# First layer of a two-layer cross attention: both turned blocks of a pair ahead of the value products, third turning bank from the start, sums read elsewhere, large loads spread

## The chip, the cores and the metric

One NeuronCore of a Trainium2 chip runs the whole program. The metric is the device time of one launch in microseconds (us). TensorE (PE) multiplies and transposes, VectorE (DVE), ScalarE (ACT) and GpSimd (POOL) do the elementwise work, SyncE (SP) issues nearly all the transfers. TensorE's clock is granted at one of two levels, 1.2 or 2.4 GHz, and the trace tells which.

## The reference

Two sequences (B = 2) of 512 tokens by 512 features attend to 1024 context tokens each. First comes a grouped-query layer with 32 query heads, 8 key/value heads and a head size of 16:

```python
q = hidden @ Wq + bq; k = enc @ Wk + bk; v = enc @ Wv + bv
scores = einsum('bkgld,bksd->bkgls', q, k) * scale + mask
out = einsum('bkgls,bksd->bkgld', softmax(scores), v)
x = out @ Wo + bo + hidden          # then layer norm, gamma, beta
```

Then follow two cross attentions of 16 heads of size 128 with layer norms and an MLP of 2048. The change touches only the first, grouped-query layer and the transfers that run beside it.

## The kernel before

The kernel is one program with its order written out by hand for every engine; semaphores tie the engines together. Each of the two sequences ("batch" in the code) passes through three stages: projections of the first layer, its attention loop, and then the two large attentions and the MLP. The loop of the first layer begins 36.0 us after the span's start and the first output product (L1269) ends it at 288.4 us; for the second sequence these are 1335.2 and 1588.7 us.

**The attention loop.** It has 128 steps (STEPS0). A step is 128 query rows of two key/value heads stacked in the row halves of the array against 1024 context tokens. 8 steps are a unit (UNIT), 4 steps a group (GROUPS), 2 steps a pair. For each step t:

- `scores0(r)` (L1193) makes the scores of steps 2r and 2r+1 into the two 2-bank tiles `ps_s[0]` and `ps_s[1]`. It first waits for `max0_done`, that is until DVE has read both tiles of the pair before.
- `maxima0(t)` on DVE (L1676) adds the mask, writes `sm` and takes the row extreme.
- `exp0(t)` on ACT (L815) writes `p0` and the row sum.
- `turned0(t)` on PE (L1212) transposes the 128x1024 block in 16 row-tiled pieces of 64 rows into two PSUM banks, half q=0 and half q=1. Three banks are there for it (`turn_banks`: `ps_t[0]`, `ps_t[1]`, `ps_m[1]`), and `bank_of_half` deals them out in turn. Before it starts, PE waits for both its banks to have been copied out (`t0_copied`).
- `copied0(t, q)` copies a half from PSUM to `pt0`: q=0 on ACT (L723 in the trace, a helper), q=1 on DVE (L1684).
- `values0` (L1229) multiplies the turned blocks of a whole group by V, in quarters i = 0 to 3, two quarters in each pair, for the group before the one being turned.

At the end of a unit PE also transposes the inverse sums (L1236), ACT copies them (`rb0`, L723), and DVE's `normalised(u)` (L1696) writes `aT0`; the next unit's first value product waits for that (`a0_done`).

**The order in one pair (t odd, r = (t-1)/2).** PE: `scores0(r+1)`, `turned0(t-1)`, two quarters of `values0`, `turned0(t)`. DVE: `maxima0(t+1)`, at one place `normalised`, `maxima0(t+2)`, `copied0(t-1,1)`, `copied0(t,1)`. ACT: `copied0(t-1,0)`, `exp0(t+1)`, `copied0(t,0)`, `exp0(t+2)`, and once a unit the copy of the inverse sums. In the first four steps (`h < UNIT`) only two of the three banks are used, since `ps_m[1]` still holds a part of the query projection (`bank0[5]`), which DVE evacuates with `low_part(5)` in step t = 1.

**Queues beside it.** SP issues, in order: the scratch writes and stack reads of q and k, then `x_res` (1 MB) and a row, `w0o` (1 MB), `acc` (0.5 MB), and the 16 `wob` tiles (0.5 MB each, two buffers), of which the third waits for POOL's sums. POOL adds the row to `x_res` in unit 2 and then scales and sums the `wob` tiles (`value_rows`, as many in a unit as `ROWS_OF_UNIT` says); each unit it also spreads the inverse sums (L613).

Of the kernel before, what the change touches and what calls it, by code (L numbers as in the profile page):

```python
# [29 lines left out]
KVH, GROUPS, HD = 8, 4, 16  # L30
# [14 lines left out]
UNIT = 2 * GROUPS  # L45
UNITS0 = KVP * LT
STEPS0 = UNITS0 * UNIT
# [4 lines left out]


P_Q = (2, 3, 4, 5)
ROWS_OF_UNIT = (0, 0, 0, 1, 1, 1, 2, 1, 1, 2, 1, 1, 2, 1, 1, 1)
assert sum(ROWS_OF_UNIT) == LAYERS * PAIRS and len(ROWS_OF_UNIT) == UNITS0
U_PROJ0, U_MLP = 6, 2 * FPAIRS
U_B = U_PROJ0 + LT + U_MLP
# [30 lines left out]
def build(nc, d):  # L89

    with ExitStack() as ctx:
# [142 lines left out]
        bank_free = sem("bank_free")  # L234
# [7 lines left out]
        w0o_in = sem("w0o_in")  # L242
# [43 lines left out]

        rows1 = (row, row1)

        bank0 = [ps_m[0][:], ps_m[1][:], ps_s[0][:, 0:512], ps_s[1][:, 0:512], ps_m[0][:], ps_m[1][:]]
        turn_banks = [*ps_t, ps_m[1]]  # L290
        bank_of_half = [h % 2 if h < UNIT else (0, 1, 2, 0, 2, 1, 0, 2)[h % 8] for h in range(2 * STEPS0)]

        def half0(t, q):

# [11 lines left out]
        def inverse0(u):  # L306

            return ps_m[0][:, u % 2 * 2 * P + P:u % 2 * 2 * P + 2 * P]
# [51 lines left out]
        def _(sp):  # L360
# [8 lines left out]
            def load_wob(b, f):  # L369
                if f >= 2:  # L370
                    sp.wait_ge(acc_done, (b * V_B + f - 1) * 2)
                    apart()
                sp.dma_start(wob[f % 2][:], d["wo"][f, :, :, :]).then_inc(wob_in[f % 2], 16)
# [28 lines left out]
            def batch(b, last):  # L402
# [12 lines left out]
                for i in range(4):  # L415
# [11 lines left out]
                    if i == 1:  # L427
                        for k in range(2):
                            sp.wait_ge(scr_k_out[k], 16 * (b + 1))
                            apart()  # L430
                            stack_k(sp, k, slice(1, KVP), stack_rest)

                sp.dma_start(x_res[:], d["x"][b, :, :, :]).then_inc(xres_in, 16)
                load_row(b * ROWS, 0)
                sp.dma_start(w0o[:], d["w0o"]).then_inc(w0o_in, 16)

                def load_wv(f):
                    load_vo(b * VO_B + 2 * f, d["wv"][f, :, :].rearrange("p (s n) -> p s n", s=2))
# [8 lines left out]
                def move_turned(x, m):  # L447
# [5 lines left out]
                    for j in range(4):  # L453
                        for a in range(4):
                            sp.dma_start(f32(pT[1][32 * a:32 * a + 32, j, :]),  # L455
                                         pb[32 * j:32 * j + 32, a, :]).then_inc(moved_in[j], 16)

                sp.dma_start(acc[:], d["rows1"]).then_inc(acc_in, 16)
                for f in range(V_B):
                    load_wob(b, f)  # L460
                load_wqk(0)
                load_wv(0)
# [59 lines left out]
        def _(pool):  # L522
# [63 lines left out]
            def batch(b, last):  # L586
# [11 lines left out]

                u0 = b * UNITS0
                for u in range(UNITS0):  # L600
                    if u == 2:
                        pool.wait_ge(xres_in, 16 * (b + 1))
                        pool.wait_ge(row_in, 16 * (2 * b + 1))
                        add_row()
                        pool.wait_ge(acc_in, 16 * (b + 1))
                        pool.wait_ge(const_in, 16 * 5)
                    for i in range(ROWS_OF_UNIT[u]):
                        value_rows(sum(ROWS_OF_UNIT[:u]) + i)

                    pool.wait_ge(rz0_done, u0 + u + 1)  # L610
                    if u >= 2:
                        pool.wait_ge(rb0_filled, u0 + u - 1)
                    nc.gpsimd.tensor_tensor(r0[u % 2][:], rz0[:, u % 2, :].unsqueeze(2).to_broadcast([P, UNIT, HD]),  # L613
                                            zero[:].unsqueeze(2).to_broadcast([P, UNIT, HD]), ALU.add)\
                        .then_inc(r0_done, 1)
# [105 lines left out]
        def _(act):  # L721
            def copy(out, in_):
                return nc.scalar.activation(out, in_, ACT.Copy)  # L723
# [60 lines left out]
            def batch(b, last):  # L784
# [22 lines left out]
                def exp0(t):  # L807
                    u, i = t // UNIT, t % UNIT
                    if t >= 2:
                        act.wait_ge(t0_filled[1], t0 + t - 1)  # L810
                    if t % UNIT == 0 and u >= 2:
                        act.wait_ge(rz0_done, b * UNITS0 + u - 1)
                    act.wait_ge(max0_done, t0 + t + 1)
                    col = i % GROUPS * 2 + i // GROUPS
                    nc.scalar.activation(p0[t % 2][:], sm[t % 2][:], ACT.Exp, bias=nm0[:, t % 2:t % 2 + 1],  # L815
                                         scale=-1.0, accum_out=z0[:, u % 2, col:col + 1]).then_inc(exp0_done, 1)
# [11 lines left out]
                for t in range(1, STEPS0, 2):  # L828
                    copied0(t - 1, 0)
                    if t + 2 < STEPS0:  # L830
                        exp0(t + 1)
                    copied0(t, 0)
                    if t + 2 < STEPS0:
                        exp0(t + 2)
                    if t % UNIT == GROUPS - 1 and t > UNIT:
                        u = t // UNIT - 1
                        act.wait_ge(rb0_filled, b * UNITS0 + u + 1)
                        copy(rb0[u % 2][:], inverse0(u)).then_inc(rb0_done, 1)
                act.wait_ge(rb0_filled, b * UNITS0 + UNITS0)
                copy(rb0[1][:], inverse0(UNITS0 - 1)).then_inc(rb0_done, 1)  # L840
                act.wait_ge(row_added, b * ROWS + 2)
# [224 lines left out]
        def _(pe):  # L1066
# [23 lines left out]
            def free(n):  # L1090
                pe.wait_ge(bank_free, n + 1)
# [23 lines left out]
            with pe.Fori(0, B) as b:  # L1115
# [29 lines left out]
                def project_q0(i):  # L1145
                    if i == 0:
                        pe.wait_ge(batch_done, b + 1)
                    if i >= 2:
                        free(nb + i)
                    for c in range(CT):  # L1150
                        mm = passes(bank0[P_Q[i]], lambda x, _: query_weights(x, i)[:, c, :],
                                    lambda y, _: hT[y][:, c, :], 1, start=c == 0, stop=c == CT - 1)
                    mm.then_inc(bank_filled, 1)
# [22 lines left out]


                pe.wait_ge(stack_in, 16 * 18 * (b + 1))
                pe.wait_ge(bank_free, nb + 6)
                pe.wait_ge(v32_done, b * 3 + 3)  # L1180
                apart()

# [17 lines left out]
                def turned0(t):  # L1200
                    pe.wait_ge(exp0_done, t0 + t + 1)
                    for q in range(2):
                        before = half_before(t, q)
                        if before is not None:
                            pe.wait_ge(t0_copied[before[1]], t0 + before[0] + 1)
                        elif bank_of_half[2 * t + q] == 2:
                            pe.wait_ge(bank_free, nb + U_PROJ0 + 2)
                    apart()
                    for st in range(ST):
                        for q in range(2):  # L1210
                            rows = slice(TILE * q, TILE * q + TILE)
                            mm = nc.tensor.transpose(half0(t, q)[:, st * TILE:(st + 1) * TILE],  # L1212
                                                     p0[t % 2][rows, st * P:(st + 1) * P], ident[rows, rows])
                            if st == ST - 1:
                                mm.then_inc(t0_filled[q], 1)
# [27 lines left out]
                for r in range(1, PAIRS0):  # L1243
                    t = 2 * r + 1
                    if r + 1 == PAIRS0 // KVP:
                        pe.wait_ge(stack_rest, 16 * 30 * (b + 1))
                    if r + 1 < PAIRS0:
                        scores0(r + 1)
                    turned0(t - 1)
                    if t >= GROUPS:  # L1250
                        for i in (t % GROUPS - 1, t % GROUPS):
                            values0(t // GROUPS * GROUPS - GROUPS, i)
                    turned0(t)
                for i in range(4):
                    values0(STEPS0 - GROUPS, i)

# [278 lines left out]
        def _(dve):  # L1535
# [8 lines left out]
            def apart():  # L1544

                dve.sem_inc(apart_dve, 1)
# [89 lines left out]
            def batch(b, last):  # L1636
# [21 lines left out]
                    low_part(i)  # L1658
                for i in range(2):
                    values_in(i)  # L1660
                for i in range(3, 5):
                    low_part(i)


# [28 lines left out]
                def normalised(u):  # L1693
                    kp, lt = divmod(u, LT)
                    dve.wait_ge(rb0_done, u0 + u + 1)
                    nc.vector.tensor_tensor(aT0[:, kp, lt * P:(lt + 1) * P], unit0(u), rb0[u % 2][:],  # L1696
                                            ALU.mult).then_inc(a0_done, 1)
# [3 lines left out]
                for t in range(1, STEPS0, 2):  # L1701
                    if t + 1 == UNIT:
                        dve.wait_ge(mask_rest, 16 * (b + 1))
                        apart()
                    if t + 2 < STEPS0:
                        maxima0(t + 1)
                    if t % UNIT == GROUPS + 1 and t > UNIT:
                        normalised(t // UNIT - 1)
                    if t + 2 < STEPS0:
                        maxima0(t + 2)  # L1710
                    copied0(t - 1, 1)
                    copied0(t, 1)
                    if t == 1:
                        low_part(5)
                    if t % UNIT == UNIT - 1:
                        inverse(t // UNIT)
                normalised(UNITS0 - 1)
# [333 lines left out]
```

## Time and profile before

| | |
|---|---|
| Runs before (3) | 2613.81, 2618.31, 2618.70 us; median 2618.31 |
| Profiled execution | 2616.33 us, of which the span is 2614.3 us |
| Busy share of the span | PE 96%, weight loads 79%, DVE 65%, ACT 57%, POOL 50% |
| Mean granted TensorE clock | 0.989 of full |

Busy shares are averages over stages with different limits: in the large attentions PE hardly pauses, in the first layer it does. The page is therefore read by stage.

### The profile page before, as it was taken

The page shows a single profiled execution, that of the slowest core. Times are in us where ns is not written, and L with a number is a line of the kernel's source. Part 1 is how long each engine was busy: PE and PEld are TensorE (multiplying, and loading weights), DVE is VectorE, ACT ScalarE, POOL GpSimd, SP SyncE. Part 2 cuts the span into 40 slices and gives each one's busy share as a digit, 9 for nine tenths or more (in the row PEclk, how much of TensorE's full clock was granted, in tenths as well). Part 3 has the DMA queues.
Part 4 walks back from the last instruction along what each step waited for, and adds up shares of the span by engine and source line. Part 5 has one row for each costly group of instructions (what it writes and reads, how often), then busy time and mean ns, then how long its engine had stood idle before and what let it go on. Part 6 is the DMA issues. An engine that isn't in the chain of part 4 may idle for free. (4 is left out here: it accounts for less than half of the span.)

```text
span 2614.3 us, 53032 instructions
## 1 busy us (share of the span) xinstructions
PE 2497.5 (96%) x19480; PEld 2063.8 (79%) x19480; DVE 1711.2 (65%) x2600; ACT 1495.2 (57%) x2360; POOL 1310.0 (50%) x746
## 2 busy tenths in 40 slices
PE   6888999999999999999978889999999999999999
PEld 5666688888888888888866666888888888888887
DVE  5999776656657656665269996665666576666541
ACT  5899455555445555545458994555554555554543
POOL 1244246666544666555603433466655446665644
PEclk8999999999999999999989999999999999999999
DMA  7312125354423445442472110334545133544522
GB/s 216 92 58 69 34 71 127 98 124 131 101 73 83 115 103 132 118 113 70 153 173 76 53 67 33 94 104 112 130 111 121 52 99 99 126 128 103 132 71 64
DMA packets 83649, 263.57 MB, mean 101 GB/s; under 512 B 20096, under 2 KB 24336, under 8 KB 77088
## 3 DMA queue, kind: packets, MB, share of 16 engines
q1 hardware_dynamic: 82496, 260.80, 37.6%
q8 instruction: 114, 1.87, 0.3%
q10 hardware_dynamic: 992, 0.52, 0.1%
q14 instruction: 47, 0.39, 0.0%
HBM read 135.39 MB, written 8.40 MB: 55 GB/s over the span
## 5 line engine op out<-in xcount | busy, mean ns | idle before, releaser
L537 POOL TENSOR_TENSOR pT_lo<-pT_lo,pT_hi 128x1024 fp32r<-128x1024 f32 x220 | 529.2, 2406 | 502.2 <-ACT pT_hi L723 496.3
L723 ACT ACTIVATE pT_hi<-pT_lo 128x1024 fp32r<-128x1024 f32 x224 | 237.8, 1062 | 327.4 <-DMA pT_lo<-pb 327.4
L862 ACT ACTIVATE p<-ps_s,nm 128x1024 f32<-128x1024 f32 x256 | 284.7, 1112 | 205.5 <-DVE nm L1755 204.9
L1752 DVE TENSOR_REDUCE nmx<-ps_s 128x1 f32<-128x1024 f32 x256 | 309.7, 1210 | 121.9 <-PE ps_s L1071 121.9
L1071 PE MATMUL ps_s<-kT,qT 128*128 128x512 f32 x1536 | 383.6, 392 | 0.0
L1771 DVE STREAM_TRANSPOSE pb<-p 128x1024 f32<-128x1024 f32 x224 | 278.2, 1242 | 105.8 <-ACT p L862 101.6
L1071 PEld LDWEIGHTS ps_s<-kT,qT 128*128 128x128 f32 x1536 | 281.3, 188 | 55.4 <-ACT p L862 1.0
L1676 DVE CUSTOM_DVE_ANT_0 sm<-ps_s,mask 128x1024 f32<-128x1024 f32 x256 | 305.4, 1213 | 19.5 <-PE ps_s L1193 15.5
L815 ACT ACTIVATE p<-sm,nm 128x1024 f32<-128x1024 f32 x256 | 293.2, 1145 | 19.1 <-DVE nm L1676 15.3
L1071 PE MATMUL ps_t<-ctxT,wa 128*128 128x512 f32 x1080 | 255.9, 390 | 0.0
L1071 PE MATMUL ps_m<-hT,wa 128*128 128x512 f32 x1008 | 243.5, 393 | 0.7 <-ACT g L1033 0.7
L1071 PEld LDWEIGHTS ps_t<-ctxT,wa 128*128 128x128 f32 x1080 | 202.9, 188 | 43.1 <-issue 1.0
L537 POOL TENSOR_TENSOR wa<-stg_qk,wa 128x1024 fp32r<-128x1024 f32 x80 | 190.8, 2403 | 70.3 <-ACT wa L723 70.2
L1071 PEld LDWEIGHTS ps_m<-hT,wa 128*128 128x128 f32 x1008 | 187.4, 188 | 46.3 <-issue 7.0
L1071 PEld LDWEIGHTS ps_t<-wv,ctxT 128*128 128x128 f32 x1728 | 212.7, 188 | 6.9 <-DVE pT_lo L1761 1.1
L1071 PE MATMUL ps_t<-wv,ctxT 128*128 128x256 f32 x1728 | 215.6, 280 | 0.0
L1212 PE MATMUL ps_t<-ident,p 64*128 64x64 f32 x2608 | 188.0, 235 | 17.6 <-DVE pt L1684 10.9
L1212 PEld LDWEIGHTS ps_t<-ident,p 64*128 64x128 f32 x2608 | 154.9, 145 | 57.8 <-issue 54.0
L613 POOL TENSOR_TENSOR r<-rz,zero 128x128 f32<-128x128 f32 x32 | 12.7, 398 | 352.9 <-issue 223.6
L537 POOL TENSOR_TENSOR v<-proj,v 128x512 fp32r<-128x512 f32 x128 | 164.8, 1298 | 40.9 <-ACT v L723 40.6
L1229 PE MATMUL ps_m<-pt,v 128*32 128x128 f32 x4096 | 142.9, 280 | 37.4 <-DVE aT L1696 29.9
L1336 PE MATMUL ps_m<-pT_hi,v 128*128 128x512 f32 x512 | 163.8, 391 | 2.9 <-POOL pT_lo L537 2.4
(181 smaller groups left out, 4664.2 us busy)
## 6 DMA issues: line engine op xcount, KB each, us to landing
pT_lo<-pb SPq DMA_DIRECT2D x896, 128.0 KB, 2.3
stg_qk<-in_wqk SPq DMA_DIRECT2D x40, 1024.0 KB, 7.4
stg_vo<-in_wo SPq DMA_DIRECT2D x48, 512.0 KB, 3.6
wob<-in_wo SPq DMA_DIRECT2D x32, 512.0 KB, 3.6
stg_vo<-in_wv SPq DMA_DIRECT2D x32, 512.0 KB, 3.6
q_stack<-scr_q SPq DMA_DIRECT2D x48, 128.0 KB, 4.2
st_ctx<-in_ctxT SPq DMA_DIRECT2D x8, 512.0 KB, 6.2
scr_q<-parts SPq DMA_DIRECT2D x8, 512.0 KB, 6.2
```

The lines of the kernel that those rows point to most:

```text
L537: return nc.gpsimd.tensor_tensor(out, x, f32(hi), ALU.subtract)
L613: nc.gpsimd.tensor_tensor(r0[u % 2][:], rz0[:, u % 2, :].unsqueeze(2).to_broadcast([P, UNIT, HD]), zero[:].unsqueeze(2).to_broadcast([P, U ...
L723: return nc.scalar.activation(out, in_, ACT.Copy)
L815: nc.scalar.activation(p0[t % 2][:], sm[t % 2][:], ACT.Exp, bias=nm0[:, t % 2:t % 2 + 1], scale=-1.0, accum_out=z0[:, u % 2, col:col + 1]) ...
L862: nc.scalar.activation(p[t % 2][:], ps_s[t % 2][:], ACT.Exp, bias=nm[:, i:i + 1], scale=SCALE1, accum_out=sums[:, i:i + 1]).then_inc(exp_d ...
L1071: mm = nc.tensor.matmul(out, lhs(x, c), rhs(y, c), start=start and c == 0 and i == 0, stop=stop and c == n_tiles - 1 and i == 2)
L1212: mm = nc.tensor.transpose(half0(t, q)[:, st * TILE:(st + 1) * TILE], p0[t % 2][rows, st * P:(st + 1) * P], ident[rows, rows])
L1229: mm = nc.tensor.matmul(unit0(u)[gr * 2 * HD:(gr + 1) * 2 * HD, :], v32[:, st, 2 * kp + gr % 2, cols_v], pt0[(t + gr) % RING][:, st, :], s ...
L1336: mm = nc.tensor.matmul(bank1(n)[:].rearrange("p (j n) -> p j n", j=4), v[a][:, st, h * P:(h + 1) * P], moving[c](st), start=st == 0 and i ...
L1676: nc.vector.tensor_tensor_reduce(sm[i][:], ps_s[i][:], mask[:, lt, :], -1.0, 3.0e38, ALU.add, ALU.min, nm0[:, i:i + 1]).then_inc(max0_done, 1)
L1752: nc.vector.tensor_reduce(nmx[:, i:i + 1], ps_s[t % 2][:], AX.X, ALU.max, negate=True)\
L1771: nc.vector.transpose(pb[:].rearrange("p a (s n) -> p s a n", s=ST)[:, :, :, lt * 32:(lt + 1) * 32], p[t % 2][:].rearrange("p (s a n) -> p ...
```

## The change

- The parts of the query projection that were made in `ps_m[0]` and `ps_m[1]` (`bank0[4]`, `bank0[5]`) are made in the second halves of `ps_s[0]` and `ps_s[1]`. The loop's first scores wait for all six parts to be read, `low_part(5)` moves ahead of the loop, and all three turning banks are used from the first step.
- PE turns both blocks of a pair one after the other and then does the value products.
- `normalised(u)` and ACT's copy of the inverse sums are placed in another round of the loop: `normalised` one pair earlier, after the copies, and the ACT copy ahead of `exp0(t+2)`.
- SP holds `x_res` and its row back until 4 groups are done, `acc` and the first `wob` until 6, the second `wob` until 7, and `w0o` goes between the fourth and the fifth `wob`. POOL adds the row in unit 3 and its sums are dealt out a little later.

```diff
-ROWS_OF_UNIT = (0, 0, 0, 1, 1, 1, 2, 1, 1, 2, 1, 1, 2, 1, 1, 1)
+ROWS_OF_UNIT = (0, 0, 0, 0, 1, 1, 2, 1, 2, 1, 2, 1, 2, 1, 1, 1)
-        bank0 = [ps_m[0][:], ps_m[1][:], ps_s[0][:, 0:512], ps_s[1][:, 0:512], ps_m[0][:], ps_m[1][:]]
+        bank0 = [ps_m[0][:], ps_m[1][:], ps_s[0][:, 0:512], ps_s[1][:, 0:512],
+                 ps_s[0][:, 512:1024], ps_s[1][:, 512:1024]]
-        bank_of_half = [h % 2 if h < UNIT else (0, 1, 2, 0, 2, 1, 0, 2)[h % 8] for h in range(2 * STEPS0)]
+        bank_of_half = [(0, 1, 2, 0, 2, 1, 0, 2)[h % 8] for h in range(2 * STEPS0)]
...
+                def after_group(n):
+                    sp.wait_ge(pv0_done, b * (STEPS0 // GROUPS) + n)
+                    apart()
+
+                after_group(4)
                 sp.dma_start(x_res[:], d["x"][b, :, :, :]).then_inc(xres_in, 16)
                 load_row(b * ROWS, 0)
-                sp.dma_start(w0o[:], d["w0o"]).then_inc(w0o_in, 16)
...
+                after_group(6)
                 sp.dma_start(acc[:], d["rows1"]).then_inc(acc_in, 16)
                 for f in range(V_B):
+                    if f == 1:
+                        after_group(7)
+                    if f == 4:
+                        sp.dma_start(w0o[:], d["w0o"]).then_inc(w0o_in, 16)
                     load_wob(b, f)
...
-                    if u == 2:
+                    if u == 3:
                         pool.wait_ge(xres_in, 16 * (b + 1))
...
                     copied0(t, 0)
-                    if t + 2 < STEPS0:
-                        exp0(t + 2)
                     if t % UNIT == GROUPS - 1 and t > UNIT:
                         u = t // UNIT - 1
                         act.wait_ge(rb0_filled, b * UNITS0 + u + 1)
                         copy(rb0[u % 2][:], inverse0(u)).then_inc(rb0_done, 1)
+                    if t + 2 < STEPS0:
+                        exp0(t + 2)
...
-                    if i >= 2:
-                        free(nb + i)
...
-                pe.wait_ge(bank_free, nb + 6)
+                pe.wait_ge(bank_free, nb + U_PROJ0 + 2)
...
                     turned0(t - 1)
+                    turned0(t)
                     if t >= GROUPS:
                         for i in (t % GROUPS - 1, t % GROUPS):
                             values0(t // GROUPS * GROUPS - GROUPS, i)
-                    turned0(t)
...
-                for i in range(3, 5):
+                for i in range(3, 6):
                     low_part(i)
...
-                    if t % UNIT == GROUPS + 1 and t > UNIT:
-                        normalised(t // UNIT - 1)
                     if t + 2 < STEPS0:
                         maxima0(t + 2)
                     copied0(t - 1, 1)
                     copied0(t, 1)
-                    if t == 1:
-                        low_part(5)
+                    if t % UNIT == GROUPS - 1 and t > UNIT:
+                        normalised(t // UNIT - 1)
```

## Rows read from the trace of the kernel before

**Rows 1.** Stretches: us from:to, length, busy us (count) by engine, PE clock, DMA.

```profile
119.70:134.30 14.60, 12.58 (x275) 9.27 (x273) 14.38 (x26) 13.50 (x26) 4.83 (x4) 1.00 0.12 39
...
36.00:288.40 252.40, 210.36 (x4373) 154.60 (x4374) 232.14 (x417) 218.14 (x401) 81.75 (x65) 0.95 0.29 79
1335.10:1588.70 253.60, 210.81 (x4373) 155.24 (x4374) 231.91 (x417) 218.32 (x401) 81.79 (x65) 0.95 0.29 79
```

**Rows 2.** Order of time, DVE: start us, us, engine, line, operation, count, [idle before].

```profile
119.71 0.69 DVE L1684 COPY pt<-ps_t 128x512 f32<-128x512 f32 x1 [0.18 <-PE ps_t L1212]
...
126.30 1.28 DVE L1684 COPY pt<-ps_t 128x512 f32<-128x512 f32 x2
...
129.79 0.68 DVE L1684 COPY pt<-ps_t 128x512 f32<-128x512 f32 x1
...
132.12 0.28 DVE L1696 TENSOR_TENSOR aT<-ps_m,rb 128x128 f32<-128x128 f32 x1
...
134.33 0.69 DVE L1684 COPY pt<-ps_t 128x512 f32<-128x512 f32 x1 [0.18 <-PE ps_t L1212]
```

**Rows 3.** Order of time, TensorE: scores, turned blocks and value products at full clock.

```profile
59.47 0.73 PE L1193 MATMUL ps_s<-k_stack,q_stack 48*128 48x512 f32 x4
60.27 0.71 PE L1212 MATMUL ps_t<-ident,p 64*128 64x64 f32 x16
...
127.88 1.08 PE L1229 MATMUL ps_m<-pt,v 128*32 128x128 f32 x32
128.90 0.33 PE L1236 MATMUL ps_m<-ident,r 128*128 128x128 f32 x1
...
133.48 0.27 PE L1212 MATMUL ps_m<-ident,p 64*128 64x64 f32 x1
...
134.98 0.24 PE L1212 MATMUL ps_m<-ident,p 64*128 64x64 f32 x1 [0.27 <-issue]
...
135.62 1.08 PE L1229 MATMUL ps_m<-pt,v 128*32 128x128 f32 x32
```

**Rows 4.** Order of time, ACT, the same stretch.

```profile
134.28 0.60 ACT L723 ACTIVATE pt<-ps_m 128x512 f32<-128x512 f32 x1 [0.74 <-PE ps_m L1212]
```

**Rows 5.** Who waited for whom, 90 to 270 us: us in total, times, longest.

```profile
PE ps_m L1229 <- DVE aT L1696: 11.9, 12, 1.0
```

**Rows 6.** Order of time, TensorE at half clock, first pairs and just behind the stall.

```profile
44.55 1.12 PE L1212 MATMUL ps_t<-ident,p 64*128 64x64 f32 x16 [2.65 <-DVE pt L1684]
...
51.46 1.23 PE L1193 MATMUL ps_s<-k_stack,q_stack 48*128 48x512 f32 x4
52.72 1.11 PE L1212 MATMUL ps_t<-ident,p 64*128 64x64 f32 x16
53.77 1.08 PE L1229 MATMUL ps_m<-pt,v 128*32 128x128 f32 x16
...
79.74 1.93 PE L1229 MATMUL ps_m<-pt,v 128*32 128x128 f32 x32
81.60 0.37 PE L1212 MATMUL ps_m<-ident,p 64*128 64x64 f32 x1
```

**Rows 7.** Order of time, ACT at the loop's start.

```profile
41.93 0.60 ACT L723 ACTIVATE pt<-ps_t 128x512 f32<-128x512 f32 x1 [0.89 <-PE ps_t L1212]
...
53.84 0.60 ACT L723 ACTIVATE pt<-ps_t 128x512 f32<-128x512 f32 x1 [0.37 <-PE ps_t L1212]
```

**Rows 8.** Order of time, TensorE at the one long stall.

```profile
76.22 0.64 PE L1229 MATMUL ps_m<-pt,v 128*32 128x128 f32 x2 [2.95 <-issue]
```

**Rows 9.** Stretches around the stall and around 1577 us, columns as in Rows 1.

```profile
76.00:78.00 2.00, 1.78 (x20) 1.40 (x22) 0.00 (x0) 0.01 (x1) 0.00 (x0) 0.50 0.98 401
...
1578.00:1580.00 2.00, 2.00 (x40) 1.53 (x34) 1.37 (x3) 0.77 (x2) 0.00 (x0) 0.50 0.00 0
```

**Rows 10.** Order of time, TensorE at the end of the loop.

```profile
276.11 0.73 PE L1193 MATMUL ps_s<-k_stack,q_stack 48*128 48x512 f32 x4
...
288.37 13.90 PE L1269 MATMUL ps_m<-w0o,aT 128*128 128x512 f32 x32
```

More of the change, by code:

```diff
@@ L1205, in turned0 @@
                             pe.wait_ge(t0_copied[before[1]], t0 + before[0] + 1)
-                        elif bank_of_half[2 * t + q] == 2:
-                            pe.wait_ge(bank_free, nb + U_PROJ0 + 2)
                     apart()
```

## The prediction

> **What bounds the kernel now.** The change touches only the first layer's loop, so the page's shares (PE 96% over the span) say nothing about it. I read the table of stretches first: the two loops take 252.4 and 253.6 us, together 506 of 2614 [rows 1]. In a steady unit of 8 steps DVE is busy 14.38 of 14.60 us, ACT 13.50, PE 12.58 [rows 1]. So DVE sets the pace there, ACT is close and PE has the most room. The order of time on DVE confirms it. A unit runs from the copy at 119.71 to the copy at 134.33, that is 14.62 us. An undisturbed pair is 129.79 - 126.30 = 3.49 us (two copies start 0.60 apart, two maxima 1.15 apart) [rows 2]. Four such pairs make 13.96; with the reciprocal of the sums (about 0.12) and the normalising step (start to start 0.21, busy 0.28 [rows 2]) a unit needs 14.29. DVE therefore waits some 0.33 us in each unit, and all of it lies in the pair behind `normalised`, where PE has stood 1.0 us waiting for `a0_done`, 12 times in the steady stretch [rows 5].
>
> Three things are lost outside the steady units. With two banks, the second turned block waits 2.65 us for a DVE copy [rows 6], and one pair later it happens again. At 73.3 us PE stands still for 2.95 us with nothing to wait for that the trace shows, while the transfers move some 400 GB/s, and its clock is then granted at 0.50, that is 1.2 GHz, for about 7 us [rows 8, 9]. And the first 19 us of the loop run at 1.2 GHz: a turned block takes 1.11 us there and 0.71 later [rows 3, 6].
>
> **The changed order on PE, the largest term.** What has to be asked is what `turned0(t)` waits for. With the pattern (0, 1, 2, 0, 2, 1, 0, 2), two blocks turned together need four halves and only three banks exist. For every odd t the half q=1 gets the very bank that the half q=0 of t-1 has just used: half 3 takes bank 0 again behind half 0, half 7 takes bank 2 behind half 4. So the second block of a pair always waits until ACT has copied a half of the first one. Before, two quarters of the value products (1.08 us) lay between the two blocks and covered that round trip. Now nothing does, and the value products come behind it.
>
> The chain of one pair at full clock, start to start:
> - scores to the first turned block: 60.27 - 59.47 = 0.80 [rows 3]
> - that block to ACT's copy of it: 134.28 - 133.48 = 0.80, a case where ACT was waiting [rows 3, 4]
> - the copy to the next turned block: 134.98 - 134.28 = 0.70 (0.60 of copy and 0.10 of signal) [rows 3, 4]
> - the turned block to the value products: 135.62 - 134.98 = 0.64 [rows 3]
> - the value products to what follows: 128.90 - 127.88 = 1.02, with 1.08 busy [rows 3]; I take 1.05 for the scores that follow now.
>
> The sum is 3.99 us. Without the round trip it was 0.80 + 0.64 + 1.05 + 0.76 = about 3.25, below DVE's 3.49. At 3.99 PE's chain is the longest. DVE needs 3.49 and ACT 3.24 (two copies at 0.49 start to start, two exponentials at 1.13, which run without a gap in most pairs), so ACT is free when the first block is ready and adds nothing, and the two row maxima of a pair are read 3.3 us after its scores began, before the 3.99 are over. Once a unit the transpose of the inverse sums adds 0.26 start to start (0.33 busy [rows 3]). A unit is 4 x 3.99 + 0.26 = 16.22 us against 14.62: +1.6.
>
> The link from value products to scores occurs nowhere in the trace. Its lower bound is a start 0.2 before the last products end; its upper bound is their whole 1.08 and the 0.09 that stand between the scores' end and the next block (0.80 less 0.71). With the other links the pair comes to 3.8 to 4.1.
>
> **The sums in another round.** ACT's copy of the inverse sums (0.15 start to start) and `normalised` (0.21) keep their cost. The wait of 1.0 us for `a0_done` [rows 5] goes: `normalised` is done about 5 us after the pair's scores, and the value product that needs it starts 7 us after them. This would be worth the 0.33 us a unit if DVE were the bound. PE being the bound, it is already in the chain above, which holds no such wait. ACT now waits for the transpose ahead of `exp0(t+2)`, about 1 us; ACT has 0.75 us a pair to spare, and `exp0(t+2)` is asked for only 1.5 us after the next pair's first block. Cost nothing; with no cover, at most 0.3 us a unit.
>
> **Third bank at once.** The second block then starts behind ACT's copy (41.93 + 0.70 = 42.6) and not at 44.55 [rows 6, 7]. The third pair's scores start when DVE has read the second pair, about 0.9 us (a copy and its signals) before that 44.55: at 43.7. From there the chain without value products, 1.26 + 1.12 + 0.70 and about 0.85 from the second block to the scores (links below), brings the fourth pair's scores at 47.6 and not at 51.46 [rows 6]: 3.9 us won, 0.7 of them from `low_part(5)`, which goes to before the loop, where DVE waits for the stack transfer anyway. But from there the new order works against it. At 1.2 GHz a pair's chain is 1.26 (51.46 to 52.72) + 1.12 (52.72 to 53.84) + 0.70 + 1.05 (52.72 to 53.77) + 1.86 (79.74 to 81.60) = 5.99 us [rows 6, 7]. If the clock rises where it did, 19 us in, the fifth pair starts at 53.6 and the sixth pair's scores start at about 58.3 against 59.47 [rows 3]: 1.2 us ahead. The waits of the query projection that fall away were met already, and the loop's first scores wait for the stack transfer as before: 0.
>
> **Loads set apart.** The stall costs 2.95 us [rows 8], and the half clock behind it about 1.8 more: a pair of the old order then takes PE some 5.0 us (1.26 + 1.05 + 1.86 and about 0.85 [rows 6]) against DVE's 3.49, for a little over one pair. Together 4.7 in each loop. With 1.25 MB in flight at a time and not 3.5 this goes; the chain above counts none. The new SP waits hold back only loads: POOL's 16 sums of 4.5 us fit in 12 units, and the last tile goes out in the same unit as before. Bounds: 0 to 4.7 stay.
>
> **The tail.** Before, the last scores (276.11) to the first output product (288.37) is 12.3 us [rows 10]. There both blocks of the last pair now come before its products; the chain gives 11.0, 1.3 less.
>
> **The sum.** First loop: from the sixth pair's scores at 58.3, 58 pairs x 3.99 + 15 x 0.26 = 235.3 gives 293.6, plus 11.0 is 304.6 against 288.4: +16.2 us. Second loop, with the same length of 268.6 against 253.5 (1335.2 to 1588.7) [rows 1]: +15.1. The sum is +31.3 on the profiled 2616.3: 2647.6. The median of the runs lies 2 us above the profiled one. I say 2648.
>
> **Rivals.**
> (1) Faster: the round trip costs nothing, because value products fill it or ACT answers early, and DVE stays the bound. Per loop: 3.9 at the start, 4.7 of stall, 14 x 0.33 of waits and 1.3 at the tail, 14.5 us in all; 2587. It decides at a PE chain of 3.49. For it speaks that DVE is the bound today; against it that the wait stands in the code ahead of both halves and that copy and signal were 0.70 wherever the next block stood ready. "TensorE: Matmul & The Clock Gate" (the Trainium skill, Part 3) says that matmuls keep their order and only weight loads are pulled ahead, so the products could not slip in front.
> (2) The same: the chain is near 3.7, if the link to the scores and the round trip overlap by 0.3; then about 17 us a loop of the loss are gone: 2614.
> (3) Much slower: the clock falls inside the loop. It fell once in a stretch without a stall, at 1577.6 [rows 9], behind a stretch in which PE was held up for `a0_done`. Each fall of 7 us costs a little over 2 us in the new chain; with one fall in every second unit, 2665 to 2685. Against it: the long gap between value products goes. The same page (Part 1, on PSUM-queue cycling) tells of a kernel whose clock swung because PE paused briefly between groups, which is what the new order does.
> (4) It doesn't do what it says: the stall moves to another load and stays, +4.7 a loop: 2657.
>
> **Chances.** The chain with its bounds (3.8 to 4.1 us, clock rising 7 us earlier or later, stall gone or not) 0.76, own range 2632 to 2662. Rival 1 0.13, rival 2 0.06, rival 3 0.05; rival 4 is inside the first. I draw the range to 2614 below and 2668 above, leaving rival 1 and most of rival 3 out. A measurement of this kernel tells 0.2% (5 us) from no change. Faster by more 0.14, within 0.04, slower by more 0.82.
>
> **What would show it.** Right: in a steady unit DVE's busy share falls from 98% to about 89%; scores start 4.0 us apart; the second turned block starts 0.70 behind ACT's copy and idles for ACT; no wait for `a0_done` is left; no gap of 3 us on PE near 73 us. Wrong: scores 3.5 us apart with DVE without gaps (rival 1), or a granted clock of 0.5 within the steady stretch (rival 3).

## The result and the profile after

The changed kernel takes 2637.12 us (median of 4 runs, 2635.98 to 2637.78) beside 2616.26 us before (4 runs): a ratio of 1.0079, with a 95% interval of 1.0062 to 1.0097. It is slower by some 21 us. The forecast was 2648 (2614 to 2668), slower; the direction and its mechanism came true, the size was half as large again as the measured one (some 31 us where 21 were measured).

The table of stretches of the kernel after. The columns are those of [rows 1]; the rows are one steady unit, the two loops, and the two microseconds around what is left of the stall:

```profile
120.20:135.80 15.60, 11.75 (x277) 9.61 (x273) 14.70 (x27) 13.97 (x27) 4.81 (x4) 1.00 0.28 103
...
35.90:300.50 264.60, 198.06 (x4373) 160.33 (x4374) 235.62 (x416) 224.74 (x401) 81.79 (x65) 0.96 0.28 76
1345.00:1609.80 264.80, 197.91 (x4373) 160.40 (x4374) 235.59 (x417) 225.00 (x402) 81.72 (x65) 0.95 0.28 77
...
68.00:70.00 2.00, 1.64 (x23) 1.19 (x22) 0.46 (x2) 0.96 (x2) 0.00 (x0) 1.00 1.05 191
```

Against [rows 1], a unit of 8 steps takes 15.6 us and not 14.6, for the same work: DVE, which set the pace before with 0.2 us of idle time, is now idle for 0.9 us, and TensorE is busy 11.75 us where it was 12.58. From the first scores to the first output product the two loops take 264.5 and 263.3 us, where they took 252.4 and 253.5: 21.9 us in all. The spans differ by 20.9 us (2635.2 against 2614.3), so the two loops hold the whole of the loss.

Two pairs in order of time, first TensorE, then ScalarE (start us, us, engine, line, operation, count, [idle before]); in this kernel L1201 are the scores, L1218 the turned blocks, L1235 the value products, L733 ScalarE's copies:

```profile
126.17 0.24 PE L1218 MATMUL ps_m<-ident,p 64*128 64x64 f32 x1 [0.94 <-ACT pt L733]
...
126.81 1.08 PE L1235 MATMUL ps_m<-pt,v 128*32 128x128 f32 x32
127.82 0.73 PE L1201 MATMUL ps_s<-k_stack,q_stack 48*128 48x512 f32 x4
128.39 0.22 PE L1218 MATMUL ps_t<-ident,p 64*128 64x64 f32 x1
...
130.00 0.24 PE L1218 MATMUL ps_t<-ident,p 64*128 64x64 f32 x1 [0.94 <-ACT pt L733]
```

```profile
129.15 0.60 ACT L733 ACTIVATE pt<-ps_m 128x512 f32<-128x512 f32 x1
```

The first block of the pair starts at 128.39, ScalarE copies its half from 129.15, and only then, at 130.00, does the second block start, after TensorE has stood idle for 0.94 us. From 126.17 to 130.00 a pair takes 3.83 us. Who waited for whom between 90 and 285 us (us in total, times, longest):

```profile
PE ps_m L1218 <- ACT pt L733: 24.9, 25, 1.2
PE ps_t L1218 <- ACT pt L733: 23.8, 25, 1.2
```

Each of the 50 second blocks of this stretch waits about 0.97 us for ScalarE, 48.7 us in all. Before, the rows of this kind came to 1.4 us in the same stretch; the wait of value products for the normalised sums [rows 5] is gone from the list. The stall of 2.95 us [rows 8] has shrunk to 1.29 us (in the second loop from 2.67 to 0.74 us), and behind it the clock doesn't fall: once it has risen (at 59.6 us in the first loop), it stays at 2.4 GHz in both loops. ("issue" marks a wait that the profile ties to no other engine.)

```profile
68.36 0.38 PE L1235 MATMUL ps_m<-pt,v 128*32 128x128 f32 x2 [1.29 <-issue]
```

### The profile page after: what moved, and what is told of

Same layout as the page of the kernel before. It is cut to its first block, busy times and chain, and to the rows that moved or that the text cites. A ratio compares the mean times of both kernels' runs of the same rounds, so it can differ in the third digit from the quotient of the medians.

```text
span 2635.2 us, 53034 instructions
## 1 busy us (share of the span) xinstructions
PE 2472.7 (94%) x19480; PEld 2074.2 (79%) x19480; DVE 1719.7 (65%) x2600; ACT 1508.3 (57%) x2360; POOL 1311.0 (50%) x746
## 4 chain that ended last, share of the span: by engine, by line
PE 79%; ACT 8%; issue 4%; DVE 4%; DMA 2%; SPq 1%; POOL 1%; ACTq 0%; DVEq 0%; POOLq 0%
PE ps_m L1081 20%; PE ps_t L1081 18%; PE ps_s L1081 15%; PE ps_m L1342 6%; PE ps_t L1342 6%; PE ps_m L1235 4%; ACT p L825 3%; ACT pt L733 3%; PE ps_t L1218 2%; PE ps_s L1201 2%; PE ps_m L1218 2%; POOL pT_lo L547 1%; SPq L460 1%; PE ps_m L1275 1%; PE ps_m L1091 1%
## 5 line engine op out<-in xcount | busy, mean ns | idle before, releaser
L733 ACT ACTIVATE pT_hi<-pT_lo 128x1024 fp32r<-128x1024 f32 x224 | 237.8, 1062 | 328.9 <-DMA pT_lo<-pb 328.9
L1218 PE MATMUL ps_t<-ident,p 64*128 64x64 f32 x2560 | 179.1, 229 | 60.9 <-ACT pt L733 58.8
L1218 PEld LDWEIGHTS ps_t<-ident,p 64*128 64x128 f32 x2560 | 162.6, 143 | 79.1 <-issue 69.3
L1218 PE MATMUL ps_m<-ident,p 64*128 64x64 f32 x1536 | 135.4, 231 | 63.7 <-ACT pt L733 62.3
L1218 PEld LDWEIGHTS ps_m<-ident,p 64*128 64x128 f32 x1536 | 119.0, 143 | 78.7 <-issue 72.3
```

## The experiments

The theory (A) is this: what costs is TensorE's order alone. With three banks the second block of a pair cannot start before ScalarE has copied a half of the first, and the value products, which used to fill that round trip, now stand behind it. The other parts gain. The rivals are given with each run.

### One part undone: the old order in the changed kernel

```diff
                     turned0(t - 1)
-                    turned0(t)
                     if t >= GROUPS:
                         for i in (t % GROUPS - 1, t % GROUPS):
                             values0(t // GROUPS * GROUPS - GROUPS, i)
+                    turned0(t)
```

> The changed kernel with one thing undone: the two quarters of value products stand between the two turned blocks of a pair again. Theory A (the second block waits for ScalarE's copy of the first, and the products that covered that wait now come behind it): the pair falls from 3.82 us to VectorE's own 3.5 to 3.6, a unit to 14.3 to 14.5, and the gains of the other parts show: 2592 to 2602 us, faster than the kernel before. Rival B (the loss comes from another part, the third bank, the sums' new place or the late loads): it stays at 2630 to 2640.

Measured: 2591.38 us (5 runs), beside 2619.18 before; ratio 0.9899, interval 0.9883 to 0.9916. That is just under theory A's span and far from rival B's. The same kernel again, e11 below, gave 2588.52. So these few lines are worth about 46 us, and the rest of the change is a gain of 28. A steady unit, and TensorE's waits between 90 and 270 us (this loop ends at 273.9):

```profile
119.00:133.30 14.30, 12.93 (x276) 9.48 (x277) 14.30 (x27) 13.67 (x26) 4.92 (x5) 1.00 0.31 112
```

```profile
PE ps_s L1201 <- DVE nm L1682: 9.1, 29, 0.6
...
PE ps_m L1218 <- ACT pt L733: 2.0, 4, 1.2
```

DVE is busy all of the 14.30 us, TensorE waits for DVE, and the wait for ScalarE's copy is 2.3 us (2.0 in this row, 0.3 in another) where the changed kernel has 44.9 us between 90 and 270 us. Starts of scores are 3.49, 3.55, 3.48 and 3.68 us apart, 14.20 a unit. This version beats both kernels.

### The new order alone, in the kernel before

> The kernel before with the new order on TensorE alone (both blocks turned, then the products). Theory A: pairs of 3.82 to 3.9 us in place of 3.65, and the stall of 3 us and the two-bank waits stay: 2640 to 2655 us. Rival B: within 5 us of the kernel before, 2616. Rival C (the new order helps and something else hurts): under 2611.

The edit is the one above, the other way round. Measured: 2644.64 us (6 runs) beside 2619.18; ratio 1.0102, interval 1.0085 to 1.0119. The wait appears at once, in the same size as in the changed kernel:

```profile
PE ps_m L1212 <- ACT pt L723: 23.9, 25, 1.2
PE ps_t L1212 <- ACT pt L723: 23.8, 25, 1.2
```

It lies in theory A's span; rivals B and C are out. The order costs 25 us on the kernel before and 46 us on the kernel that has the other parts. A part of the difference shows in the units. With the new order a unit takes 15.54 us with the sums in their old place (here) and 15.63 in their new one (the changed kernel). With the old order it takes 14.61 and 14.20. The new order thus not only adds its wait, it also takes away what the sums' move is worth.

### The large loads alone

> The kernel before with the large loads set apart alone (transfers held back until 4, 6 and 7 groups are done, the row added in unit 3). Theory A (the 2.95 us stall of TensorE near 73 us and the half clock behind it come from the code transfer that stands behind 3.5 MB of loads): both go, 4 to 5 us in each loop, 2606 to 2609 us. Rival B (the stall has another cause): it stays, 2614 to 2618. Rival C (the late loads make GpSimd late): slower than 2620.

The edit is SP's and POOL's part of the diff. Measured: 2612.53 us (12 runs) beside 2619.18; ratio 0.9978, interval 0.9967 to 0.9988: 6 us faster, less than the 8 to 10 of theory A and outside its span, but clear of no change. The 2.95 us stall is gone from the trace; what is left are waits of 0.62 us at 66.8 us and 0.96 at 89.5, and of 0.89 at 1364.2 in the second loop. But the clock is granted at 1.2 GHz again for 3.4 us from 69.1 us, and three times more in the second loop (from 1366.2, 1427.6 and 1458.3 us, for 3.4 to 6.8 us), which takes a part back.

That the loads make the stall is not shown by this. Its length changes with the loads where they were: 2.95 and 2.67 us in the two loops of the kernel before, 1.14 and 1.40 with the new order alone, 1.94 and 1.41 with the third bank alone, 1.57 and 2.40 with the sums alone; in e10 below the first loop has none and the second 2.20. With the loads spread it is 1.61 and 1.54 in e11. What ends the wait stands in no row.

### The third bank alone

> The kernel before with the third bank from the first step alone. Theory A: the two waits of 2.65 and 2.85 us for VectorE's copy go, 3 to 4 us in each loop: 2608 to 2612 us. Rival B: the fourth pair is earlier but the clock rises later by one stretch of 3 to 7 us and takes it back: 2614 to 2618.

The edit is the bank lists, the waits on `bank_free` and the place of `low_part(5)`. Measured: 2606.57 us (6 runs) beside 2619.18; ratio 0.9957, interval 0.9940 to 0.9973: 11 us by the ratio and 13 by the medians, more than the 3 to 4 in each loop that theory A gave it, and below its span. The second block starts at 42.70, with 0.73 us of idle before it, and not at 44.55 with 2.65 [rows 6]:

```profile
42.70 0.34 PE L1209 MATMUL ps_m<-ident,p 64*128 64x64 f32 x1 [0.73 <-issue]
```

The fourth pair's scores come 11.5 us after the first and not 15.5. The clock rises 3 to 4 us earlier than before, counted from each loop's first scores, so rival B, which had it rise later, was wrong in its sign. Later in the first loop it is granted at 1.2 GHz three times more, for 3.4 us each (from 59.2, 113.9 and 144.6 us), in the second loop not again. So the first loop is 1.4 us shorter than before and the second 7.4 us (250.96 and 246.10 us). How much of the gain is the banks' and how much the clock's and the stall's isn't taken apart.

### The sums in their other round alone

> The kernel before with the sums in their other round alone (the copy of the inverse sums ahead of the second exponential, the normalising step one pair earlier). Theory A: one pair in each unit takes 4.07 us because TensorE waits for the normalised sums; it falls to about 3.68, 0.39 us in each of 14 units of both loops: 11 us, and fewer falls of the clock: 2603 to 2609 us. Rival B (VectorE and ScalarE only trade places of the same wait, as the exponential is late now): 2614 to 2620.

The edit is the two moved blocks on ACT and DVE. Measured: 2601.72 us (5 runs) beside 2616.18; ratio 0.9938, interval 0.9924 to 0.9951: 14 us, the largest of the three gains by the medians, and more than theory A's 11 (2603 to 2609). The three alone add to 34 us by the medians; together, in e1, they are worth 28. The unit's fourth pair goes from 4.07 to 3.68 us, 0.40 us in each unit, and no row of value products waiting for the normalised sums [rows 5] is left. A steady unit:

```profile
119.00:133.30 14.30, 12.90 (x286) 9.47 (x281) 14.30 (x27) 13.63 (x26) 4.83 (x4) 1.00 0.14 39
```

### One quarter of the products between the blocks

```diff
                     turned0(t - 1)
+                    if t >= GROUPS:
+                        values0(t // GROUPS * GROUPS - GROUPS, t % GROUPS - 1)
                     turned0(t)
                     if t >= GROUPS:
-                        for i in (t % GROUPS - 1, t % GROUPS):
-                            values0(t // GROUPS * GROUPS - GROUPS, i)
+                        values0(t // GROUPS * GROUPS - GROUPS, t % GROUPS)
```

> The changed kernel with one quarter of the value products between the two turned blocks and one behind the second. Theory A: the round trip through ScalarE (0.76 for the block, 0.85 from the copy to the next block, 1.61 in all) covers the first quarter wholly, TensorE's chain is 0.57 + 1.61 + 0.64 + 0.5 = 3.3 us, under VectorE's 3.49: as fast as the old order, 2588 to 2598 us. Rival B (what costs is each change between turning and value products, of which there are now four in a pair and not two): slower than the old order by over 5 us, 2600 or more.

Measured: 2599.34 us (5 runs) beside 2616.18; ratio 0.9933, interval 0.9919 to 0.9946. It recovers about 38 of the 46 us with half of the products moved back. The wait for ScalarE between 90 and 270 us is down from 44.9 to 21.3 us:

```profile
PE ps_m L1218 <- ACT pt L733: 10.9, 24, 0.6
PE ps_t L1218 <- ACT pt L733: 10.4, 25, 0.6
```

The time lies just above the span that theory A gave, and it is 8 to 11 us above the old order (2591.38 and 2588.52), which is what rival B asked for. "TensorEngine Tiling (Array Packing)" (the Trainium skill, Key Properties) says that changing the tiling mode drains the engine; this version has four such changes a pair (turning by row tiles, products by column tiles) where the other two orders have two. No run here shows the drain by itself. The 8 to 11 us are less than 0.09 us for each of the 128 pairs, which bounds two further changes; they can't be split here between drains and the waits left. So rival B is bounded, not excluded; and as the new order has no more changes than the old one, it can't explain the 46 us.

### ScalarE's copy made later, in both orders

```diff
                     act.wait_ge(t0_filled[q], t0 + t + 1)
+                    if t % 2 == 0:
+                        copy(spare[:], ones[:].unsqueeze(1).to_broadcast([P, 2, P]))
                     copy(pt0[t % RING][:, :, TILE * q:TILE * q + TILE], ...
```

> The changed kernel with an extra ScalarE copy of 256 columns in front of its copy of each pair's first block, about 0.3 us from start to start. Theory A (the round trip through ScalarE is on the chain that sets the pair): every pair grows by the whole of it, some 3.82 to 4.1 us, 2660 to 2678 us. Rival B (TensorE's own work or its changes of mode set the pair, ScalarE has 0.6 us to spare): no change, 2630 to 2642.

> The same extra ScalarE copy in the kernel that has all of the change but the order (value products between the turned blocks). Theory A: the products cover most of the round trip; TensorE's chain grows to 3.4 to 3.5, ScalarE's own work to about 3.5, beside VectorE's 3.5: 2591 to 2603 us, so that the delay costs a third of what it costs in the new order or less. Rival B (ScalarE is the bound here): the full 0.3 us a pair, 2625 or more.

Measured beside 2616.18 before: in the new order 2675.78 us (5 runs; ratio 1.0220, interval 1.0206 to 1.0234), in the old order 2595.51 (5 runs; ratio 0.9919, interval 0.9906 to 0.9933). The added copy takes 0.32 us from start to start. In the new order it adds 39 us over the changed kernel, which is 0.30 for each of the 128 pairs. In the old order it adds 4 to 7. Both are in theory A's spans. The new order, ScalarE and then TensorE:

```profile
125.06 0.42 ACT L734 ACTIVATE spare<-ones 128x256 f32<-128x256 f32 x1 [0.43 <-PE ps_m L1221]
125.38 0.58 ACT L734 ACTIVATE pt<-ps_m 128x512 f32<-128x512 f32 x1
```

```profile
126.21 0.24 PE L1221 MATMUL ps_t<-ident,p 64*128 64x64 f32 x1 [1.24 <-ACT pt L734]
```

and the old order, the same place:

```profile
125.75 0.24 PE L1221 MATMUL ps_m<-ident,p 64*128 64x64 f32 x1 [0.52 <-ACT pt L734]
```

In the new order ScalarE is waiting (0.43 us) when the block comes, takes its extra copy, and TensorE's idle time grows from 0.94 to 1.24: whatever is added to the round trip is added to the pair. In the old order the products take up most of it. So the round trip sets the pair in one order and is mostly covered in the other.

### What the spread loads are worth in the other kernels

> The changed kernel with the loads, GpSimd's dealing of sums and its row addition where they were before. Theory A: the stall of TensorE near 70 us comes back and with it the half clock, 2 to 5 us in each loop: 2641 to 2647 us. Rival B: since in the new order the pairs are longer, the code transfer is in time anyway: within 3 us of the changed kernel, 2634 to 2640.

> The kernel with the third bank and the sums' other round, but with the order and the loads of before. Theory A: it lacks what the spread loads gave the kernel before (6.6 us): 2595 to 2600 us. Rival B: the shift of the pairs alone moves the code transfer out of the loads: equal to the one with the spread loads, 2588 to 2594.

> The kernel with all of the change but TensorE's order, once more, beside the one without the spread loads on the same chip: 2588 to 2594 us, as measured before; the difference of the two is what the spread loads are worth.

Measured beside 2617.72 before: the changed kernel with the old loads 2643.69 us (4 runs; ratio 1.0102, interval 1.0084 to 1.0120). The old order with the old loads took 2592.54 (6 runs; 0.9902, 0.9887 to 0.9918), and with the spread ones 2588.52 (4 runs; 0.9892, 0.9875 to 0.9909). In the new order the spread loads save some 6 us: 2643.69 lies in theory A's span, and no run of the one kernel reaches those of the other, though the intervals of the two ratios (the changed kernel's is 1.0062 to 1.0097) overlap a little. Two stalls stand in the trace where the changed kernel has one of 1.29 us:

```profile
76.71 0.81 PE L1226 MATMUL ps_m<-pt,v 128*32 128x128 f32 x18 [1.09 <-issue]
...
85.78 1.08 PE L1226 MATMUL ps_m<-pt,v 128*32 128x128 f32 x32 [1.65 <-issue]
```

In the old order the difference of 4 us lies within the intervals. The time of the old order with the old loads, 2592.54, is in rival B's span and under theory A's, and its first loop has no stall at all; but 4 us can't be told from nothing here, so it isn't decided.

One more thing stands in these numbers. The changed kernel with the old loads has the new order, the third bank and the sums' new place, and its ratio is that of the new order alone, 1.0102 both times. The two parts that gained 11 to 13 and 14 us alone in the old order gain nothing together in the new one. The start does come sooner (the fourth pair's scores 11.3 us after the first, not 15.4), but the units are 0.09 us longer; what else takes it back isn't taken apart.

## Why the prediction was right, and where its sizes were off

**What bounds the loop.** Right: DVE bound the kernel before with one wait a unit, and the old order with that wait removed runs DVE without a gap, 14.20 us a unit where the prediction had put DVE's need at 14.29.

**The changed order.** The step that carried the forecast was right: each second block waits for ScalarE's copy of the first. Its terms were mis-sized. The trace of after has 3.83 us a pair and not 3.99:
- scores to first block: 0.57 (127.82 to 128.39), not 0.80. In the kernel before, that block stood behind ScalarE's copy of the block before it as well, and I read that copy's end as the scores' price. Other pairs of the kernel before have the same 0.80 (122.89 to 123.69, 126.44 to 127.24, 129.92 to 130.72), because ScalarE's copy starts beside the scores in all of them.
- block to copy: 0.76, not 0.80.
- copy to next block: 0.85, not 0.70. The second block of a pair starts 0.25 us behind the copy's end, the first one 0.10.
- block to products: 0.64, as said.
- products to scores, which no row had shown: 1.01, taken as 1.05.

A unit then takes 3.90 + 3.82 + 3.82 + 4.09 = 15.63 us, +1.0 and not +1.6. Over 14 to 15 units in two loops this term alone is 17 us of forecast too much. The whole miss is only 11 us, because other terms were too small: what is left of the stall costs 3.3 us (the two pairs that hold it took 5.73 and 5.20 us), the start 1.8, the tail 1.0, and a few single pairs are longer. That these errors partly cancel is luck.

Of the signs, DVE's share fell from 98 to 94% (14.70 of 15.60 us) and not to 89, scores start 3.8 to 4.1 us apart, the second block starts 0.85 behind the start of ScalarE's copy and not 0.70, no wait for `a0_done` is left, and no gap of 3 us.

**The sums in another round.** Priced at nothing because TensorE would be the bound, and at 0.33 us a unit if DVE were. Both were right: 0.40 a unit in the kernel before, and no gain with the new order (15.54 a unit with the sums in their old place, 15.63 in the new one).

**Third bank.** Right at the start: the fourth pair's scores were forecast at 47.6 and came at 47.45. The sixth pair's came at 59.2 and not 58.3, since the clock rose at 59.6 us and not at 55.3 as assumed; the two pairs before it took 5.88 and 5.87 us at 1.2 GHz (forecast 5.99). Why it rose later isn't shown. With the old order this part alone was worth more than had been expected of it (e4).

**Loads set apart.** Forecast to remove the whole stall: 1.29 us of it stayed in the first loop and 0.74 in the second. The gain alone is 6 us where 4.7 a loop, 9.4, had been counted, and the step from the loads to the stall is not shown (e3).

**The tail.** From the last scores to the first output product it took 11.77 us in the first loop; the forecast was 11.0, and before it was 12.3 [rows 10].

**The rivals.** Rival 1 (faster, DVE stays the bound) is what the kernel with the old order does: 2591 where 2587 was worked out. It needed the products in the gap, as the prediction said. Rival 3 (the clock falls inside the loop) didn't happen: after the rise the changed kernel has no stretch at 1.2 GHz in either loop, where the kernel before has three. With a round trip 0.3 us longer it did happen (e7, see the last section).

## What to carry to other kernels

When two stages share a ring of buffers that is one short of holding both, the second waits for a drain of the first. The place of the work that fills this wait decides more than how much of it there is: moved from the gap to behind it, one microsecond of products cost 46 us in 128 pairs, and half of it put back regained most.

A gain off the critical path is not lost but hidden: the same move of the sums was worth 14 us alone in one order, and in the other the units got no shorter by it. So undo the parts of a change one by one before dropping it.

Read the price of a link from a place where it alone ends the wait; a link that shows the same number everywhere may be measuring its neighbour.

## What the runs showed of the hardware

Where the transposes stood ready and waited for ScalarE's copy, they started 0.10 us behind its end in the first block of a pair and 0.25 in the second, in nearly all cases of every kernel that has them (126.53 + 0.60 to 127.23 and 124.91 + 0.59 to 125.75 in the old order with the delay; 129.15 + 0.60 to 130.00 in the changed kernel, whose first blocks don't wait). In the code ScalarE's signal is the first of two waits for the one and the last for the other; that this is the reason wasn't tried.

TensorE's clock was granted at 1.2 GHz for 3.4 us inside ordinary units, far from a loop's start: from 1577.6 us in the kernel before, from 1427.6 and 1458.3 with the spread loads alone, from 113.9 and 144.6 with the third bank alone. These three keep the wait of value products for the normalised sums [rows 5], of 1.03 us, and the falls lie beside it. In the changed kernel, where TensorE is busy 11.75 us of a 15.60 us unit (75%) and pauses for 0.94 us in each pair, it was granted at 2.4 GHz through both loops, once it had risen. But that wait is not needed for a fall. In the new order with ScalarE's delay (e7), which doesn't have it and pauses for 1.24 to 1.33 us in each pair, the clock fell three times in ordinary units, at 257.2, 1434.8 and 1571.4 us:

```profile
256.82 0.24 PE L1221 MATMUL ps_m<-ident,p 64*128 64x64 f32 x1 [1.33 <-ACT pt L734]
```

```profile
257.60:260.60 3.00, 3.00 (x42) 2.22 (x42) 1.15 (x2) 1.82 (x5) 0.00 (x0) 0.50 0.38 150
```

Why it fell there and not in the other units, which have the same pauses, isn't known. "TensorE: Matmul & The Clock Gate" (the Trainium skill, Part 1) tells of a kernel that swings between the levels through short pauses in each round. The changed kernel did not, with its 0.94 us in each pair; with 1.24 us it did a few times.
